# Graph network on one core: edge gathers released in two parts, index copies moved forward on ScalarE

## The reference, cut to what matters

```python
edge_index = jnp.stack([src, dst])
x = _layernorm(x + _L0_gnn_ref(x, edge_index, ...))      # three GAT layers
x = _layernorm(x + _L1_gnn_ref(x, edge_index, edge_attr_32, ...))
# one GAT layer:
h = (x @ W.T).reshape(n, heads, ch)
logits = leaky_relu(a_s[src] + a_d[dst], neg_slope)
ex = exp(logits - segment_max(logits, dst)[dst])
out = segment_sum((ex / segment_sum(ex, dst)[dst])[:, :, None] * h[src], dst)
# the edge network:
v = relu(concat([x[rol], x[col], edge_attr]) @ W1 + b1) @ W2 + b2
x = maximum(segment_max(v, col), x)
```

## Time and profile before

| | |
|---|---|
| Median of the runs | 13578.41 us |
| Span of the profiled execution | 17880.7 us |
| Busy PE, DVE, ACT, POOL in that span | 13008.3, 11518.7, 7904.7, 9819.0 us |
| Mean granted TensorE clock | 0.836 |
| Indirect DMAs of edges on POOL | 7023 in GAT, 2537 in the MLP, 944 ns each |

### The profile page before, as it was taken

One profiled execution on the slowest core, in us unless ns is written; L12 is line 12 of the kernel. 1 busy time (PEld: TensorE's weight loads), 2 busy tenths in 40 slices (PEclk: granted clock), 3 DMA queues, 4 the chain that ended last, 5 costly groups with the idle time before them and its releaser, 6 DMA issues.

```text
span 17880.7 us, 199056 instructions
## 1 busy us (share of the span) xinstructions
PE 13008.3 (73%) x48770; PEld 9273.0 (52%) x48770; DVE 11518.7 (64%) x14932; ACT 7904.7 (44%) x13203; POOL 9819.0 (55%) x10387
## 2 busy tenths in 40 slices
PE   3888888882888888883788888885466666666663
PEld 2666666662666666662566666664344444444442
DVE  4777777773777777775677777776344444444445
ACT  3555555551555555552455555553233333333331
POOL 5555555555555555555555555555544444444444
PEclk8988899885988988886888889897677777777776
DMA  2333333331222222221222222222122222222221
GB/s 79 93 95 93 95 93 96 93 96 35 66 66 66 66 66 66 67 66 37 57 66 66 66 66 66 66 66 52 56 65 67 66 64 65 67 65 66 67 65 44
DMA packets 823774, 1236.00 MB, mean 69 GB/s; under 512 B 294054, under 2 KB 449932, under 8 KB 823052
## 3 DMA queue, kind: packets, MB, share of 16 engines
q1 hardware_dynamic: 377820, 794.52, 14.7%
q0 software_dynamic: 332688, 214.90, 7.6%
q10 hardware_dynamic: 113184, 225.69, 3.4%
HBM read 882.61 MB, written 351.37 MB: 69 GB/s over the span
## 4 chain that ended last, share of the span: by engine, by line
PE 44%; issue 19%; another core or an unknown queue 17%; DVE 14%; ACT 5%; POOL 0%; DVEq 0%; ACTq 0%; DMA 0%; SPq 0%; POOLq 0%
PE bank L771 34%; PE bank L792 3%; PE bank L768 3%; ACT nodebuf L982 2%; DVE mb L1488 1%; DVE g L1453 1%; ACT oh L991 1%; DVE d_b L1499 1%; PE bank L842 1%; DVE h_sb L1463 1%; PE bank L757 1%; DVE adf L1472 1%; DVE u_sb L1595 1%; DVE s_b L1585 1%
## 5 line engine op out<-in xcount | busy, mean ns | idle before, releaser
L665 POOL DMA_INDIRECT g<-table,idx x7023 | 6626.8, 944 | 4805.8 <-ACT idx L878 2829.2
L771 PE MATMUL bank<-tab,oh 128*128 128x448 f32 x32928 | 8073.8, 399 | 235.2 <-issue 232.0
L771 PEld LDWEIGHTS bank<-tab,oh 128*128 128x128 f32 x32928 | 6573.3, 206 | 1493.0 <-issue 971.5
L665 POOL DMA_INDIRECT g<-tablex,idx x2537 | 2393.7, 944 | 2599.3 <-ACT idx L878 1803.6
L982 ACT ACTIVATE nodebuf<-nodebuf,key_at 128x512 bf16<-128x512 f32 (+1 forms) x5488 | 3363.3, 684 | 26.2 <-DMA nodebuf<-digit 0.9
L991 ACT ACTIVATE oh<-nodebuf 128x896 fp32r<-128x896 bf16 x2352 | 2172.2, 947 | 2252.0 <-remote 2126.3
L1453 DVE TENSOR_REDUCE g<-bank 128x32 f32<-128x448 f32 x2352 | 1360.9, 608 | 2474.1 <-remote 2287.4
L771 PE MATMUL bank<-tab,oh_x 128*128 128x448 f32 x8232 | 2155.0, 408 | 750.3 <-issue 749.6
L771 PEld LDWEIGHTS bank<-tab,oh_x 128*128 128x128 f32 x8232 | 1699.3, 213 | 1063.1 <-issue 940.5
L768 PE MATMUL bank<-mcoef,nodebuf 3*128 3x448 bf16 x2940 | 1131.7, 385 | 1296.2 <-DVE u_sb L1595 1067.2
L792 PE MATMUL bank<-h_sb,w_as 128*128 128x512 f32 x1176 | 910.7, 867 | 1494.7 <-issue 1341.7
(11 more groups left out here) (258 smaller groups left out, 11775.3 us busy)
## 6 DMA issues: line engine op xcount, KB each, us to landing
ad<-aux SPq DMA_DIRECT2D x4656, 64.0 KB
state<-o_sb ACTq DMA_DIRECT2D x582, 288.0 KB
nodebuf<-keys SPq DMA_DIRECT2D x588, 256.0 KB
g<-table,idx POOLq DMA_INDIRECT x7023
auxx<-wide SPq DMA_DIRECT2D x97, 1056.0 KB
xd_in<-auxx SPq DMA_DIRECT2D x194, 512.0 KB
xe_t<-in_edge_attr SPq DMA_DIRECT2D x196, 256.0 KB
vmax<-o_sb ACTq DMA_DIRECT2D x194, 256.0 KB
```

Of the source, the lines that this page charges most:

```text
L665: eng.indirect_dma_start(o, None, t[:, :], bass.IndirectOffsetOnAxis(ap=idx[k][:, j:j + 1], axis=0)).then_inc(e_g[k][j // (W // 2)], 16)
L771: last = eng.matmul(o, hot[:, b, at], tab[:, a, b, :], start=False, stop=(b == NN - 1 and a == 1))
```

## The change

On POOL, a chunk's gathers are cut at column 10 (`HALF_G`). Columns 4 to 9 (3 to 9 in the MLP) go out when the indices are there, as before. Ahead of column 10 POOL waits for a second event: in GAT for `E["red"]` to reach `4n - 8`, n being the chunk's number over all passes, which is when VectorE has reduced the last pick of chunk n-3; in the MLP for `M["pre"]` to reach `2x - 4`, x being the chunk's number in the pass, which is the second L1563 of chunk x-3. A target of zero or less is no wait. The first four chunks of pass 3 are written out ahead of the loop.

On ScalarE, the index copy stands right behind the exponentials in GAT, and right behind `rel` in the MLP.

```diff
+HALF_G = (W + SA) // 2
...
                 for j in range(SA if pass_ < 3 else SEL, count):
+                    if j == HALF_G:
+                        second_half(pass_, n)
...
+            def second_half(pass_, n):
+
+                if pass_ < 3:
+                    need(eng, E["red"], n * SA - 2 * SA)
+                else:
+                    need(eng, M["pre"], n * 2 - (3 * NC * 2 + 4))
+                tick(eng, "tickp")
+
             def gather_pass(pass_):
-                with eng.Fori(1 if pass_ == 0 else 0, NI - 1) as i:
+                if pass_ == 3:
+                    for k in range(NB):
+                        gather_edges(pass_, 3 * NC + k, k)
+                with eng.Fori(1 if pass_ in (0, 3) else 0, NI - 1) as i:
...
                     exps(i, k)
+                    if left > 1:
+                        refill(i if k + 1 < NB else i + 1, (k + 1) % NB)
                     if left > 3:
                         for c in range(SA - 1):
                             one_hot(layer, v + 3, c)
-                    if left > 1:
-                        refill(i if k + 1 < NB else i + 1, (k + 1) % NB)
...
                 rel(v)
+                if refill:
+                    need(eng, M["txs"], v * 2 + 2)
+                    next_idx(v, k)
                 if not isinstance(v, int) or v + 1 < NC:
                     rs(v + 1, 1 - b)
...
                     squares(3, v + 4, b)
-                if refill:
-                    need(eng, M["txs"], v * 2 + 2)
-                    next_idx(v, k)
```

## The result

The change makes the kernel slower by 0.44%: 13640.74 us (median of 4 runs, 13638.57 to 13643.55) against 13579.78 us (13577.87 to 13581.83), ratio 1.0044 with a 95% interval of 1.0032 to 1.0057. The difference is 61.0 us; 13632 us had been forecast.

A forecast was written before the change was run, and what follows sets the result against it. VectorE (15.6 us a chunk) was taken to lead POOL (15.0) by little in GAT, POOL to set the pace in the MLP (16.25). 63 - 3 - 6 = +54 us, from 13578.4 to 13632 us; range 13560 to 13710.

The forecast's parts named there:

- The gate at the start, +63 us: Start of pass 0: POOL waits for four reductions with 98 scatters queued behind; first scatter at about 226.5 instead of 163.45.
- The scatters, -3 us: Start of pass 0: moved to when VectorE is idle, the 98 scatters take 123.5 us instead of 126.9.
- The MLP's start, -6 us: Start of pass 3: the earlier index copy lets POOL's train of 192 chunks start 6.3 us earlier.
- The gates of the loops and the copies in GAT, 0: GAT loop: POOL's idle time only moves to before the seventh gather; ScalarE's 0.2 us copy is hidden; 0 us.
- Rival C: GAT loop: POOL restarts at the gate every chunk while being the bound; +0.4 us a chunk, 235 us, 13867; chance 0.05.
- Rival A: GAT loop: moved idle time removes 0.2 us per chunk of a remaining unexplained wait, 118 us; 13514, faster; chance 0.13.
- B: Start of pass 0: delay hidden or paid back by the loop or first pass; 13560 to 13600, same; chance 0.14.
- D: Start of pass 0: the four picks come late, TensorE slow for another reason than scatters; up to +148 us, 13717; chance 0.08.
- The starts of passes 1 and 2, 0: Scatters come first there; chunk 3's six late gathers fit in a gap of 33.65 us, so 0 us.
- The reading of the first profile: Whole span: 4115 us of VectorE waits without recorded end hardly occur in timed runs; 17880.7 less these leaves 13766 us.

The follow-up runs named there:

- three other delays: Kernel before plus the start's gate: one reduction and six gathers, four and six, four and twelve behind the wait; 49.0, 59.0 and 65.5 us over the kernel before.
- second profile of before: Kernel before, no edit, profiled again: 13580.81 us, span 13579.1 us.
- The index copies alone: Kernel before with both index copies moved as in the change and no gate: 13581.01 us, ratio 0.9999.
- the kernel without the start's gate: Whole change without the wait in the four chunks gathered ahead of node(0), against the kernel before: 13581.05 us, ratio 1.0000.
- The kernel with the scatters ahead of the gate: Whole change, gated second half of pass 0's fourth chunk issued after node(0)'s scatters: 19034.0 us (ratio 1.0436) on the slower chip, 13591.87 us (1.0001) on a faster one.
- The kernel with one reduction at the start's gate: Kernel before plus a wait for one reduced pick ahead of chunk 3's seventh gather in pass 0: 18398.59 us (ratio 1.0079) on the slower chip, 13638.59 us (1.0035) on a faster one.
- The loops' gates alone: Kernel before plus gates from the fifth chunk on in all four passes, no index copy moved: 18013.07 us on the slower chip, ratio 0.9845.
- the MLP's part alone: Kernel before with only the MLP's index copy behind rel and its gate on L1563: 13592.72 us, ratio 1.0003.

## Why the prediction was right, and which term was not

**The gate at the start, +63 us: right, place and size.** Measured 179.04 - 115.14 = 63.9 us. Both absolute times were wrong by 48 us, since the first profile had its whole start later (scatters from 163.45, against 115.14; table halves from 193.60, against 145.44), but the sum was made of distances: three picks' spacing, a reduction, the restart, six gathers. They came out as 3.3 us, 0.62, 0.79 and 7.48 us. Taking the fourth reduction from TensorE's rows and not from its own late row, 302.15, was the choice that made the number: in the kernel after it starts at 170.15. The reason given for it, that TensorE was slowed by the scatters beside it and would be free of them, does not hold at 13580 us. There the kernel before has scatters from 115.14 to 242.1 us and its four picks among them, and the last one takes its 3.11 us:

```profile
165.85 3.11 PE L771 MATMUL bank<-tab,oh 128*128 128x448 f32 x14
```

Four quick picks were forecast for a time after the scatters had moved, and at 13580 us they are quick wherever the scatters stand, so the number came right without its reason. On the slower chip the reason fits the traces, as the last section shows.

**The scatters, -3 us: right.** 126.0 to 122.5 us, and 122.5 to 122.8 us at three other delays. VectorE's last work before the picks ends at 151.5 us, ahead of all these trains and beside the undelayed one. The Trainium skill (SBUF — State Buffer, section "Who interferes with whom") has GpSimd's descriptor writes locked out while VectorE runs a copy or a tensor_scalar in its two-port mode; the trace agrees in sign, 3.6 us over 98 scatters, but no run here separates that rule from other causes. Some 1.1 of the 3.6 us fall on three scatters of 1.25 to 1.37 us from 146.66 on, beside the table halves of L1441 (145.37 to 151.3), which are a tensor_tensor and not an operation that this rule names.

**The MLP's start, -6 us: wrong, this is the step that failed.** It measured 0. The term took POOL's idle time of 36.76 us ahead of 12759.32 as part of a timed run. It was part of the long execution. In the second profile of before, the copies and the gathers stand like this (ScalarE, then POOL):

```profile
10296.15 0.20 ACT L878 ACTIVATE idx<-idx_all 128x16 int32<-128x16 int32 x1
```
```profile
10263.40 0.99 POOL L665 DMA_INDIRECT g<-tablex,idx  x1 [0.31 <-issue]
...
10328.39 0.94 POOL L665 DMA_INDIRECT g<-tablex,idx  x1 [0.30 <-issue]
```

Chunks 0 to 3 of the pass are 4 x 13 = 52 gathers, at 1.25 us each; the first of chunk 4 is therefore the one at 10328.39, and its indices had been there for 32 us. The change brings the copy forward, to 10345.90 in the kernel after, where 10296.15 + 60 = 10356 would be its old place, and POOL has no gap that could shrink. The index copies alone measured the same 0. The measured loss of 61.0 us is 7.0 us above the forecast 54: 6 are this term, the gate's is 0.9 more, the scatters' 0.6 less, and 0.7 us are left. (13632 falls 8.7 us short of 13640.7, since it was added to 13578.4 and not to 13579.8 us.)

**The gates of the loops and the copies in GAT, 0: right.** Kernel after, a chunk of pass 0:

```profile
3008.11 1.11 DVE L1467 TENSOR_REDUCE g<-bank 128x32 f32<-128x448 f32 x2
3009.48 0.94 POOL L668 DMA_INDIRECT g<-table,idx  x1 [0.94 <-DVE g L1467]
3014.65 1.02 DVE L1477 STREAM_TRANSPOSE h_sb<-g 128x512 f32<-128x512 f32 x1
3015.88 0.21 ACT L892 ACTIVATE idx<-idx_all 128x16 int32 x1
...
3025.22 0.94 POOL L668 DMA_INDIRECT g<-table,idx  x1 [1.05 <-DVE g L1467]
3030.24 1.03 DVE L1477 STREAM_TRANSPOSE h_sb<-g 128x512 f32<-128x512 f32 x1
```

The chunk takes 3030.24 - 3014.65 = 15.6 us, as forecast from the earlier trace rows less its unexplained wait, and POOL needs 15.0. The rest is idle time that POOL must spend somewhere: at the index copy before, (517.2 - 26.7) / 489 = 1.0 us each, at the gate after, (549.2 - 79.8) / 503 = 0.93 us each. Rival C was half right, the gate does bite in the loop, but on the engine that had the time. Rival A (moved idle time helps) and B (hidden, paid back) are excluded at 13580 us by the kernel without the start's gate, ratio 1.0000; D by the reduction at 170.15.

**The starts of passes 1 and 2, 0: right, but not for the reason given.** The gap of 33.65 us that was to hide chunk 3's late gathers is not there at 13580 us. In pass 1 of the kernel after, the fourth reduction ends at 3567.8, and POOL's first gather of the pass starts at 3638.53, so the gate lies in the past when POOL comes to it, and no wait of POOL longer than 0.31 us follows before 3760.

**The reading of the first profile: right on the whole, and wrong once it was forgotten.** Taking the unexplained waits out gave 13766 us for 13578; the chunk of 15.6 us was right, and so was the MLP's of 16.25 (179 chunks in 2900 us, 16.2). The prediction then used other waits of the same execution as if they were real: the 36.76 us ahead of the MLP, which made the term of -6 us, and the 33.65 us ahead of pass 1, which did no harm.

## What to carry to other kernels

A wait on an in-order engine costs what stands behind it, not what it guards: before adding one, write down the next instructions of that queue and who waits for them, above all at the start and between phases, where the queue holds other work than the loop's. The same wait passed in a loop was free on the engine with spare time, and reordering the start by one call took all of the loss away. If the profiled execution is a third longer than the timed runs, every idle time in it is suspect, not only those without a releaser.

## What the runs showed of the hardware

**One program, two chips, 13.6 and 19.0 ms.** The kernel with the scatters ahead of the gate ran on both, with the same instructions and the same 1236.01 MB. Spans and granted clocks were 13585.3 us at 0.956 and 19031.2 us at 0.822. One pick shows the difference. The slower chip (TensorE and VectorE; start, length, idle before):

```profile
3019.16 1.89 PE L789 MATMUL bank<-tab,oh 128*128 128x448 f32 x8
3021.27 1.07 PE L789 MATMUL bank<-tab,oh 128*128 128x448 f32 x4 [0.23 <-issue]
...
3022.69 0.37 PE L789 MATMUL bank<-tab,oh 128*128 128x448 f32 x1 [0.34 <-issue]
3023.40 0.47 PE L789 MATMUL bank<-tab,oh 128*128 128x448 f32 x1 [0.35 <-issue]
3023.43 0.62 DVE L1471 TENSOR_REDUCE g<-bank 128x32 f32<-128x448 f32 x1 [9.00 <-remote]
...
3030.32 2.08 PE L810 MATMUL bank<-h_sb,w_as 128*128 128x512 f32 x2 [6.45 <-DVE h_sb L1481]
```

Windows of 2 us, same chip, ahead of the chunk and around the broken pick (columns as above):

```profile
3000.00:3002.00 2.00, 0.00 (x0) 0.00 (x0) 1.36 (x4) 1.40 (x3) 0.00 (x0) 1.00 0.00 0
3002.00:3004.00 2.00, 0.00 (x0) 0.00 (x0) 1.93 (x3) 0.00 (x0) 0.00 (x0) 0.74 0.39 147
3004.00:3006.00 2.00, 0.21 (x1) 0.21 (x2) 2.00 (x3) 1.15 (x3) 0.00 (x0) 0.50 0.00 0
...
3020.00:3022.00 2.00, 1.77 (x10) 1.31 (x9) 0.00 (x0) 0.00 (x0) 1.49 (x2) 1.00 1.03 412
```

The faster chip, the same load of 418 GB/s:

```profile
3014.00:3016.00 2.00, 2.00 (x11) 1.85 (x12) 1.41 (x4) 2.00 (x4) 1.03 (x2) 1.00 1.04 418
```
```profile
3005.61 1.12 PE L810 MATMUL bank<-h_sb,w_as 128*128 128x512 f32 x2 [1.02 <-DVE h_sb L1481]
...
3013.86 3.10 PE L789 MATMUL bank<-tab,oh 128*128 128x448 f32 x14
```

On the slower chip one pick of the chunk falls apart into smaller groups with gaps of 0.23 to 0.35 us, at a granted clock of 1.00, and VectorE waits 9.00 us for it; the same pick takes 3.10 us on the other chip. TensorE then stands idle 6.45 us for VectorE. In the same stretch of the chunk before, the granted clock fell from 1.00 to 0.50 (2.4 to 1.2 GHz) while TensorE was idle, and the two matmuls behind such a gap take 2.08 us where they take 1.12 on the faster chip. So the lower clock follows from the idle time here and does not start it. The broken pick coincides with the burst of 412 GB/s; on the other chip a pick beside 418 GB/s takes its 3.10 us. In the loop no run separates the burst from something outside this core.

The start of pass 0 says more, since the experiments moved the scatters there. On the slower chip, the kernel with the scatters ahead of the gate, whose scatters run from 157.75 to 285.0 us:

```profile
253.20 0.62 DVE L1471 TENSOR_REDUCE g<-bank 128x32 f32<-128x448 f32 x1 [40.70 <-issue]
295.00 0.62 DVE L1471 TENSOR_REDUCE g<-bank 128x32 f32<-128x448 f32 x1 [41.18 <-remote]
```

The kernel with one reduction at the start's gate, same chip:

```profile
208.98 0.62 DVE L1456 TENSOR_REDUCE g<-bank 128x32 f32<-128x448 f32 x1 [2.70 <-PE bank L774]
...
211.01 1.00 POOL L635 DMA_INDIRECT aux<-td,scat_nm  x1 [0.31 <-issue]
...
213.56 0.62 DVE L1456 TENSOR_REDUCE g<-bank 128x32 f32<-128x448 f32 x1 [3.95 <-PE bank L774]
```

In the first, VectorE reduces the four picks of chunk 0 at 211.87, 253.20, 295.00 and 297.25: over 41 us apart beside the scatters, 2.3 us once they are over. The loops' gates alone, with scatters from 164.06, show the same (216.70, 257.30, 299.61, 303.49). With the scatters held back the reductions stand 3.3 to 3.6 us apart, and only the last, 2.55 us after the first scatter, comes after 4.6 us; with twelve gathers and scatters from 221.22 all four stand 3.3 us apart. So on that chip the picks at the start are slow beside scatters and quick without them, while at 13580 us they are quick beside the same scatters (159.02, 162.34, 165.67, 169.00 in the kernel before). What of the scatters does it, and why only there, stays open.

**On that chip the whole change does alter the rate of the loops.** Chunks per stretch, from the counts of one VectorE line in windows of 2000 us (transposes in pass 0, one per chunk; in the MLP, two). One reduction at the start's gate, loops as before:

```profile
1000.00:3000.00 2000.00, 102.91 (x100) 0.88 0.32 91
5300.00:7300.00 2000.00, 103.83 (x101) 0.88 0.26 65
```
```profile
15500.00:17500.00 2000.00, 123.83 (x154) 0.77 0.23 65
```

Whole change, scatters ahead of the gate:

```profile
1000.00:3000.00 2000.00, 89.53 (x87) 0.83 0.28 79
5300.00:7300.00 2000.00, 87.51 (x85) 0.83 0.21 55
```
```profile
15500.00:17500.00 2000.00, 156.00 (x196) 0.87 0.29 82
```

A chunk of GAT goes from 20.0 to 23.0 us, one of the MLP from 2000 / 77 = 26.0 to 2000 / 98 = 20.4 us. Three passes lose and one gains, 588 x 3.0 - 196 x 5.6 = some 670 us; the two spans differ by 655 us, and the runs were 770 us slower than the kernel before. So what the change moves does matter on such a chip, with both signs, as rival A supposed, though not with its sign overall. Which part of it matters is not shown. The gates alone were 1.5% faster there (ratio 0.9845), so they do not make the loss by themselves; and in GAT POOL still waits mainly for index copies under the whole change, 651.3 us in the 87 chunks between 1000 and 3000 us. The index copies alone, the MLP's part alone and the kernel after itself were not run there.
